# Routing 4,096 tokens to the two experts that they use, beside an attention pass that runs group by group

## The chip, the cores and the metric

One core of a Trainium2 chip. The time is the device time of one execution in microseconds (us), as the median of the runs. The profile is one further execution; its span runs from the first to the last instruction. Engines: PE (TensorE, with PEld for its weight loads), DVE (VectorE), ACT (ScalarE), POOL (GpSimd), SP (SyncE, which issues transfers).

## What is computed

The input x has 8 batches of 512 tokens of 128 numbers, all in float32. Cut to what matters:

```
xn = layernorm(x)
q = rope(xn @ wq);  k = rope((xn @ w_down) @ wk_up);  v = (xn @ w_down) @ wv_up     # 16 heads of 8
scores = q . k / sqrt(8), only keys whose page (32 tokens) is not later than the query's
s = softmax(scores) @ v @ wo
logits = silu(xn @ rw1 + rb1) @ rw2 + rb2          # 8 experts
w = softmax over the two largest logits, 0 elsewhere
y = xn + sum over experts e of w[e] * (silu(xn @ ew1[e] + eb1[e]) @ ew2[e] + eb2[e])   # hidden width 256
out = x + s * silu(y)
```

So only two of the eight experts have a weight that is not zero for a token.

## The kernel before

A token tile is 128 tokens, a batch has TT = 4 of them. The 16 heads form NG = 4 groups of GH = 4 heads. Every engine walks the same list of named steps in one order, and semaphores join them. The list is made of an opening, then for each of the 8 batches a stage B (`stage_b`) and a stage C (`stage_c`); steps in `AHEAD` are done for the next batch, those in `FINAL` for the one before.

Stage B is the expert half. For each of the 8 experts and both halves of the hidden width, `layer1` forms a 128x512 product as three FP32R terms (high x high, low x high, high x low, in `split_product`), ACT applies Silu into `eh`, and `layer2` multiplies each of the 4 token tiles by the second weights; DVE adds it to `acc` with the token's weight `gate_w`. All experts run on all tokens. Between them TensorE forms row scores for the softmax's maxima of groups 1 to 3 (`max_scores`), each of which DVE reduces, and turns the maxima (`neg_max_t`) so that a transfer can put them into rows of `q_stack`, where they are subtracted inside the score product. The choice of the two experts (`top_two`, `weights`) runs once per batch on DVE.

Stage C is the attention half: 12 steps of `scores` (key-major products into a ring of 4 PSUM banks), exp on ACT into `probs`, and `pv`. Around them stand the projections of the next batch (`proj`, three terms each), rope (DVE multiplies, `split` into high and low), the transfers that stack q and k (`stack` on SP), the head copies (`heads` on DVE for groups 0 and 1, `act_head` on ACT for the others) and the maxima of group 0 for the next batch (`max0`). A ring `ring` of 4 banks, two banks `wide` and two banks `misc` hold all products. POOL only forms 1/sqrt(var) and the last addition.

Of the kernel before, what the change touches and what calls it, by code (L numbers as in the profile page):

```python
# [7 lines left out]
F32R = mybir.dt.float32r  # L27
ALU = mybir.AluOpType
# [3 lines left out]
P = 128  # L32
# [10 lines left out]
NPAIR = TT * (GH // 2)  # L43
NMAX = (NG - 1) * NPAIR
NMAX0 = TT * GH
NSTEP = NG * 3
NEXP = GH // 2
# [4 lines left out]
DVE_GROUPS = 2  # L52
NACT = (NG - DVE_GROUPS) * GH
NTOP = 11
MAX_SLOT = 8
EH_RING = 6


def stage_b():

    maxima, top = iter(range(NMAX)), iter(range(NTOP))
    max_steps = (1, 1, 2, 2, 2, 2, 2, 2, 2, 2, 1, 2, 1, 1, 1, 0)
    layer2_at = {4: 0, 6: 1, 7: 2, 9: 3, 11: 4, 13: 5, 15: 6}
    extra = {0: [("logits", 0)], 1: [("gate", 0)], 2: [("out_rows", 0)], 3: [("tanh", 0), ("out_rows", 1)],
             4: [("weights", 0), ("neg_max", 0)], 5: [("out_rows", 2), ("negate", 1)],
             6: [("weights_t", 0)], 7: [("out_rows", 3)], 8: [("neg_max", 1), ("stats", 0)], 9: [("out_cols", 0)],
             10: [("negate", 2)], 11: [("project", 0)], 12: [("neg_max", 2), ("norm", 0)],
             15: [("negate", 3)]}
    seq = [("router", 0)]
    for s in range(NL1):  # L70
        seq.append(("layer1", s))
        if s == NL1 - 1:
            seq += [("x_cols", 0), ("exp_table", 0)]
        for _ in range(max_steps[s]):
            seq.append(("max", next(maxima)))
            if s >= 1:
                seq += [("top", n) for _, n in zip(range(3), top)]
        seq += extra.get(s, [])
        if s < NACT:
            seq.append(("act_head", s))  # L80
        if s in layer2_at:
            seq.append(("layer2", layer2_at[s]))
    assert not list(maxima) and not list(top)
    return seq + [("layer2", NE - 1), ("neg_max", 3), ("proj", 0), ("expert_bias", 0), ("proj", 1)]


def stage_c():

    before_pv = {5: [("heads", 0)], 8: [("heads", 1)]}
    after_pv = {0: [("proj", 2), ("split", 0), ("proj", 3)], 1: [("split", 1), ("stack", 0)], 4: [("stack", 1)],  # L90
                7: [("stack", 2)], 10: [("stack", 3)], NSTEP: [("values", 0), ("negate", 0)]}
    for n in range(NMAX0):
        at = 6 + n * 6 // NMAX0
        (after_pv if n * 6 % NMAX0 >= 12 or at == 8 else before_pv).setdefault(at, []).append(("max0", n))
    seq = []
    for n in range(NSTEP + 1):
        if n < NSTEP:
            seq.append(("scores", n))
        seq += before_pv.get(n, [])
        if n >= 1:  # L100
            seq.append(("pv", n - 1))
        seq += after_pv.get(n, [])
    return seq


STAGE_B, STAGE_C = stage_b(), stage_c()
FINAL = ("gate", "out_rows", "out_cols", "project")
AHEAD = [s for s in STAGE_B if s[0] in ("stats", "norm", "x_cols", "proj")] + [
    s for s in STAGE_C if s[0] in ("proj", "split", "stack", "values", "heads", "max0", "negate")]
MISC = ("router", "logits", "layer2", "out_rows", "out_cols", "project", "weights_t", "neg_max",  # L110
        "expert_bias", "x_cols", "proj", "values", "max0")


def opening():

    seq = [s for s in AHEAD if s[0] in ("stats", "norm", "x_cols", "proj", "values")]
    seq += [("split", 0), ("split", 1), ("stack", 0), ("stack", 1), ("stack", 2), ("stack", 3), ("router", 0),
            ("layer1", 0), ("layer1", 1), ("logits", 0)]
    top = iter(range(NTOP))
    seq += [("top", n) for _, n in zip(range(5), top)] + [("heads", 0)]  # L120
    for n in range(NMAX0):
        seq.append(("max0", n))
        if n in (3, 7):
            seq.append(("layer1", 2 + n // 4))
        if n == 7:
            seq.append(("heads", 1))
        if n >= 8:
            seq += [("top", n) for _, n in zip(range(1), top)]
    return seq + [("negate", 0)]


OPENING = opening()


def steps_of(first=False, last=False):
    return [s for s in STAGE_B + STAGE_C
            if not (first and (s[0] in FINAL or s in OPENING and s not in AHEAD)) and not (last and s in AHEAD)]


def misc_jobs(steps):  # L140

    jobs = [s for s in steps if s[0] in MISC]
    assert len(jobs) % 2 == 0
    return jobs


JOBS = {name: misc_jobs(steps) for name, steps in (
    ("prologue", OPENING), ("first", steps_of(first=True)), ("middle", steps_of()),
    ("last", steps_of(last=True)), ("epilogue", [s for s in STAGE_B if s[0] in FINAL]))}
PER_BATCH = len(JOBS["middle"])  # L150
# [4 lines left out]
def build(nc, x, wq, w_down, wk_up, wv_up, wo, rw1, rb1, rw2, rb2, ew1, eb1, ew2, eb2,  # L155
          cos_t, sin_t, ident_c, key_rows, query_rows, head_mask, rank_c, out):
    ctx = ExitStack()
    with ctx:
# [118 lines left out]
        def batch_of(step, b):  # L277

            return b - 1 if step[0] in FINAL else b + 1 if step in AHEAD else b

# [739 lines left out]
```

## Time and profile before

| | us |
|---|---|
| median of 3 runs | 667.03 (665.81 to 667.17) |
| span of the profiled execution | 663.7 |
| PE busy | 607.3 |
| DVE busy | 467.0 |
| ACT busy | 354.4 |
| POOL busy | 18.6 |

The median of the runs is 3.3 us above the profiled span, which is the part of an execution outside the first and the last instruction. Busy PE time counts pipelined products with their whole duration, so two consecutive starts say more of a product's price than its duration does. Names in the rows are cut: digits at the end of a name are left out, so `ew_sb` is `ew2_sb`.

### The profile page before, as it was taken

The page shows a single profiled execution, that of the slowest core. Times are in us where ns is not written, and L with a number is a line of the kernel's source. Part 1 is how long each engine was busy: PE and PEld are TensorE (multiplying, and loading weights), DVE is VectorE, ACT ScalarE, POOL GpSimd, SP SyncE. Part 2 cuts the span into 40 slices and gives each one's busy share as a digit, 9 for nine tenths or more (in the row PEclk, how much of TensorE's full clock was granted, in tenths as well). Part 3 has the DMA queues.
Part 4 walks back from the last instruction along what each step waited for, and adds up shares of the span by engine and source line. Part 5 has one row for each costly group of instructions (what it writes and reads, how often), then busy time and mean ns, then how long its engine had stood idle before and what let it go on. Part 6 is the DMA issues. An engine that isn't in the chain of part 4 may idle for free.

```text
span 663.7 us, 12438 instructions
## 1 busy us (share of the span) xinstructions
PE 607.3 (92%) x4116; PEld 448.6 (68%) x4116; DVE 467.0 (70%) x1199; ACT 354.4 (53%) x507; POOL 18.6 (3%) x20
## 2 busy tenths in 40 slices
PE   2569999999999999999999999999999999999895
PEld 1448855787567865678557875788656885578643
DVE  6677866787568866798667865698757875687502
ACT  2123456643766347754576438653576445763573
POOL 0000000000000100001000000001000000000000
PEclk9758999999999989999999999999999998999999
DMA  5810002100120002200021001200021001200000
GB/s 170 210 43 2 3 13 61 27 1 19 38 60 1 18 1 49 46 1 18 21 51 25 1 18 45 50 1 18 1 67 28 2 17 25 51 22 2 19 1 16
DMA packets 21798, 20.93 MB, mean 32 GB/s; under 512 B 4545, under 2 KB 14450, under 8 KB 21778
## 3 DMA queue, kind: packets, MB, share of 16 engines
q1 hardware_dynamic: 21778, 20.67, 12.9%
q8 instruction: 12, 0.20, 0.1%
q14 instruction: 8, 0.07, 0.0%
HBM read 5.45 MB, written 2.10 MB: 11 GB/s over the span
## 4 chain that ended last, share of the span: by engine, by line
PE 70%; DVE 13%; issue 12%; ACT 2%; SPq 1%; DMA 1%; DVEq 0%; POOLq 0%; POOL 0%; ACTq 0%
PE bank L500 15%; PE bank L580 10%; PE ring L517 7%; PE ring L562 7%; PE bank L446 5%; PE bank L447 5%; PE bank L448 5%; PE bank L517 5%; DVE row_max L861 5%; PE ring L565 2%; DVE acc L908 2%; PE ring L566 2%; PE bank L462 1%; ACT probs L683 1%; PE bank L478 1%
## 5 line engine op out<-in xcount | busy, mean ns | idle before, releaser
L683 ACT ACTIVATE probs<-ring 128x768 f32<-128x768 f32 (+1 forms) x192 | 158.9, 880 | 79.7 <-PE ring L562 48.8
L861 DVE TENSOR_REDUCE row_max<-ring 128x2 f32<-128x256 f32 (+1 forms) x192 | 152.3, 819 | 13.1 <-PE ring L517 13.0
L643 ACT ACTIVATE eh<-bank,bias_cols 128x512 f32<-128x512 f32 x128 | 87.8, 686 | 136.9 <-PE bank L448 134.9
L500 PE MATMUL bank<-ew_sb,eh 128*128 128x128 f32 x1024 | 125.8, 276 | 2.4 <-DVE x_lo L786 2.4
L500 PEld LDWEIGHTS bank<-ew_sb,eh 128*128 128x128 f32 x1024 | 120.1, 192 | 5.6 <-issue 3.8
L517 PE MATMUL ring<-k_head,q_stack 108*128 108x256 f32 (+2 forms) x384 | 93.4, 344 | 12.3 <-DVE row_max L861 11.2
L517 PEld LDWEIGHTS ring<-k_head,q_stack 108*128 108x128 f32 x384 | 66.7, 194 | 37.0 <-DVE row_max L861 24.8
L580 PE MATMUL bank<-probs,v_cols 128*32 128x512 f32 (+3 forms) x1024 | 88.0, 442 | 0.4 <-ACT probs L683 0.4
L908 DVE SCALAR_TENSOR_TENSOR acc<-bank,gate_w,acc 128x128 f32<-128x128 f32 x224 | 63.1, 345 | 32.3 <-PE bank L500 32.1
L856 DVE TENSOR_REDUCE row_max<-bank 128x1 f32<-128x128 f32 (+3 forms) x128 | 58.9, 487 | 32.6 <-PE bank L517 31.7
L562 PE MATMUL ring<-q_stack,k_head 128*128 128x512 f32 (+1 forms) x256 | 71.8, 395 | 3.5 <-ACT probs L683 3.5
L562 PEld LDWEIGHTS ring<-q_stack,k_head 128*128 128x128 f32 x256 | 43.1, 193 | 28.5 <-ACT probs L683 19.3
L446 PE MATMUL bank<-x_hi,ew_hi 128*128 128x512 f32 x128 | 59.4, 464 | 2.1 <-DVE bias_cols L749 2.1
L447 PE MATMUL bank<-x_hi,ew_lo 128*128 128x512 f32 x128 | 51.7, 404 | 0.0
L448 PE MATMUL bank<-x_lo,ew_hi 128*128 128x512 f32 x128 | 51.7, 404 | 0.0
L891 DVE COPY o_cols<-bank 128x512 f32<-128x512 f32 x32 | 22.1, 692 | 39.5 <-PE bank L580 39.5
L517 PE MATMUL bank<-k_head,q_stack 108*128 108x256 f32 (+2 forms) x128 | 43.1, 392 | 4.6 <-DVE k_head L884 3.0
L668 ACT ACTIVATE k_head<-k_stack,hmask 128x512 fp32r<-128x512 f32 x64 | 45.4, 712 | 0.0
L517 PEld LDWEIGHTS bank<-k_head,q_stack 108*128 108x128 f32 x128 | 24.6, 202 | 30.4 <-DVE row_max L856 18.5
L580 PEld LDWEIGHTS bank<-probs,v_cols 128*32 128x32 f32 x1024 | 23.4, 108 | 30.0 <-issue 10.5
L884 DVE TENSOR_SCALAR k_head<-k_stack,hmask 128x512 fp32r<-128x512 f32 x64 | 26.7, 482 | 13.5 <-DMA k_stack<-roped_lo 13.5
L565 PEld LDWEIGHTS ring<-q_stack,k_head 128*128 128x128 f32 x128 | 24.1, 188 | 15.1 <-ACT probs L683 15.1
(115 smaller groups left out, 659.4 us busy)
## 6 DMA issues: line engine op xcount, KB each, us to landing
k_stack<-roped_hi SPq DMA_DIRECT2D x64, 64.0 KB, 2.0
q_stack<-roped_hi SPq DMA_DIRECT2D x64, 64.0 KB, 2.0
k_stack<-roped_lo SPq DMA_DIRECT2D x32, 64.0 KB, 2.0
q_stack<-roped_lo SPq DMA_DIRECT2D x32, 64.0 KB, 2.0
out<-out_sb SPq DMA_DIRECT2D x8, 256.0 KB, 2.3
x_all<-in_L_attn_x SPq DMA_DIRECT2D x4, 448.0 KB, 6.9
probs<-in_L_ffn_ew SPq DMA_DIRECT2D x1, 1024.0 KB, 5.8
q_stack<-neg_rows SPq DMA_DIRECT2D x32, 16.0 KB
```

Of the source, the lines that this page charges most:

```text
L446: mm(ps, w_hi, x_hi[:], start=True, stop=False)
L447: mm(ps, w_lo, x_hi[:], start=False, stop=False)
L448: return mm(ps, w_hi, x_lo[:], start=False, stop=True)
L500: last = mm(ps[:, t * E:(t + 1) * E], eh[:, s % EH_RING, t * P:(t + 1) * P], ew2_sb[:, e, f, :], start=(f == 0), stop=(f == HALVES - 1))
L517: return mm(ps[:, 0:width], q_stack[0:MAX0, g, i * P:(i + 1) * P], k_head[0:MAX0, GH * g + r, 0:width], start=True, stop=True)
L562: mm(ring[:, r, j * P:T], k_head[:, h, j * P:(j + 1) * P], q_stack[:, g, j * P:T], start=True, stop=True).then_inc(st_full, 1)
L580: last = mm(wide[g % 2][32 * r:32 * r + 32, dst:T], v_cols[:, tile, GH * g + r, :], probs[:, n % 2, r, src:src + T - dst], start=(tile == ...
L643: nc.scalar.activation(eh[:, s % EH_RING, :], wide[s % 2][:], ACT.Silu, bias=bias_cols[:, s:s + 1]).then_inc(hidden_done, 1)
L683: nc.scalar.activation(probs[:, n % 2, r:r + 2, lo:T], ring[:, r:r + 2, lo:T], ACT.Exp, scale=SCALE).then_inc(exp_done, 1)
L856: V.tensor_reduce(row_max[:, 0, i, r:r + 1], ps[:, 0:(i + 1) * P], AX, ALU.max).then_inc(max0_done, 1)
L861: V.tensor_reduce(row_max[:, g, i, 2 * pair:2 * pair + 2], ring[:, 2 * (m % 2):2 * (m % 2) + 2, 0:(i + 1) * P], AX, ALU.max).then_inc(max_ ...
L908: ins = stt(out=acc[:, t, :], in0=ps[:, t * E:(t + 1) * E], scalar=gate_w[:, t, e:e + 1], in1=(xn if e == 0 else acc)[:, t, :], op0=ALU.mu ...
```

## The change

The whole order is laid out anew, with no loops in the program.

1. Attention: after an opening, 32 windows, one for each group of each batch. In a window there are three score steps; between the two halves of each stand two of the next windows' maxima (a list `MAXIMA` gives six per group, each two banks wide). The head copies, negated maxima, projections, rope and output work fill fixed places (`fills`). Six PSUM banks form one ring for nearly all products; a product waits for whoever read its banks last.
2. Projections and router are single float32 products in place of three FP32R terms.
3. All tokens are normalised, and the router runs for all 8 batches, in the opening. The choice of experts runs once for all 32 token tiles. DVE counts and TensorE sums ranks, which give each token two slots in a list of 39 tiles of 256 slots, in which a tile belongs to one expert. POOL scatters the normalised rows into it in DRAM (64 indirect transfers).
4. ACT issues transfers that pack each expert's weights and biases in DRAM and that fill the slot list with zeros first.
5. In each of the windows 9 to 18 a burst of 4 tiles runs: SP loads each tile's expert (its number read from `tile_e`) and its slots, TensorE turns them and runs both layers in float32, SP stores the results to DRAM.
6. From window 20 on POOL gathers two rows per token (64 indirect transfers), and from window 23 DVE adds them to xn with the two weights.
7. s is stored to DRAM for each batch and fetched at the end with x; silu, the product and the addition run for all batches at the end.

The diff, cut to its core:

```diff
-NPAIR = TT * (GH // 2)
-NMAX = (NG - 1) * NPAIR
-NMAX0 = TT * GH
+MAXIMA = ((0, (0, 1, 2, 3)), (1, (0, 1, 2, 3)), (2, (0, 1)), (2, (2, 3)), (3, (0, 1)), (3, (2, 3)))
+NBANK = 6
+BT = B * TT
+ROWS = 256
+NTILE = (2 * B * T + NE * (ROWS - 1)) // ROWS
+BURST = 4
+W_RING = 2 * BURST
+NBURST = -(-NTILE // BURST)
...
+def opening():
+
+    seq = [("prep", 0, 0), ("stats", 0, 0), ("norm", 0, 0), ("x_cols", 0, 0), ("proj", 0, 0), ("proj", 0, 1),
+           ("split", 0, 0), ("split", 0, 1)]
+    seq += [("stack", 0, g) for g in range(NG)]
+    seq += [("consts", 0, 0), ("router", 0, 0), ("stats", 1, 0)] + [("norm", b, 0) for b in range(1, B)]
+    seq += [("x_cols", 1, 0), ("values", 0, 0), ("logits", 0, 0), ("heads", 0, 0)]
+    for b in range(1, B):
+        seq += ([("x_cols", b + 1, 0)] if b + 1 < B else []) + [("router", b, 0)] + maximum(0, b - 1)[:b <= NM]
+        seq += [("logits", b, 0)]
...
+def window(b, g, route):
...
+    ahead = [maximum(w + 1, 4) + maximum(w + 1, 5), maximum(w + 2, 0) + maximum(w + 2, 1),
+             maximum(w + 2, 2) + maximum(w + 2, 3)]
...
+    if burst == -1:
+        seq += [("load", i, k) for i in (0, 1) for k in tiles_of(i)]
+    if GATHER_FROM <= w < GATHER_FROM + B:
+        seq.append(("gather", w - GATHER_FROM, 0))
+    for k, fill in enumerate(fills(b, g)):
...
+        seq += [("scores", b, 2 * n)] + ahead[k][0:1] + [("scores", b, 2 * n + 1)] + ahead[k][1:2]
...
+    if run:
+        seq += [("silu_table", burst, 0), ("layer1", burst, 0), ("layer1", burst, 1), ("layer2", burst, 0),
+                ("layer2", burst, 1), ("exp_table", burst + 1, 0), ("store_rows", burst, 0)]
+        if burst + 2 < NBURST:
+            seq += [("load", burst + 2, k) for k in tiles_of(burst + 2)]
...
+            def load(burst, k):
+
+                if k == 0:
+                    sp.wait_ge(s_pack, 16 * 6)
+                    sp.wait_ge(tiles_ready, 1)
+                    sp.wait_ge(scattered, 16 * 2 * BT)
...
+                expert = sp.value_load(tile_e[0:1, k:k + 1], min_val=0, max_val=NE - 1)
+                sp.dma_start(w_ring[:, k % W_RING, :],
+                             w_pack[bass.ds(expert, 1)].rearrange("o p w -> (o p) w")).then_inc(w_in_ring[k % W_RING], 16)
...
+            def proj(b, which):
...
+                for term in range(2):
+                    last = mm(ps[:, term, :], w_att[:, 2 * which + term, :], x_col[:, b % 2, :], start=True, stop=True)
...
+            def layer1(burst, q):
...
+                for c in halves_of(burst, q):
+                    for f in range(HALVES):
+                        last = mm(ps[:, c % 2, f * ROWS:(f + 1) * ROWS], w_ring[:, BURST * (burst % 2) + c, f * P:(f + 1) * P],
+                                  slots_t[:, c * ROWS:(c + 1) * ROWS], start=True, stop=True)
...
+            def consts(b, n):
+
+                act.dma_start(w_pack[:, :, 0:HID], ew1).then_inc(s_pack, 16)
...
+                act.wait_ge(prep_pool, 2)
...
+                for a in range(0, per, ZERO):
+                    n = min(ZERO, per - a)
+                    act.dma_start(flat[:, a:a + n], blank[:, 0:n]).then_inc(zeroed, 16)
...
+            def norm(b, n):
...
+                for t in range(TT * b, TT * b + TT):
+                    last = activation(xn[:, t, :], x_all[:, t, :], ACT.Identity, scale=rstd[:, t:t + 1],
+                                      bias=shift[:, t:t + 1])
...
+            G.memset(v_cols[:], 0.0).then_inc(prep_pool, 1)
+            G.memset(probs[:], 0.0).then_inc(prep_pool, 1)
...
+            def scatter(b, n):
+
+                pool.wait_ge(place_ready, 1)
+                pool.wait_ge(zeroed, 16 * -(-(NTILE * ROWS // P * E) // ZERO))
+                pool.wait_ge(xn_ready, B)
+                for t in range(BT):
+                    for which in range(2):
+                        G.indirect_dma_start(slot_rows, bass.IndirectOffsetOnAxis(ap=place[:, which, t:t + 1], axis=0),
+                                             xn[:, t, :], None).then_inc(scattered, 16)
```

## Rows read from the trace of the kernel before

**Rows 1.** The page: busy us and share of each engine; tenths in 40 slices.

```profile
PE 607.3 (92%) x4116; PEld 448.6 (68%) x4116; DVE 467.0 (70%) x1199; ACT 354.4 (53%) x507; POOL 18.6 (3%) x20
...
PE   2569999999999999999999999999999999999895
...
PEclk9758999999999989999999999999999998999999
```

**Rows 2.** The page's chain that ended last, shares by engine.

```profile
PE 70%; DVE 13%; issue 12%; ACT 2%; SPq 1%; DMA 1%; DVEq 0%; POOLq 0%; POOL 0%; ACTq 0%
```

**Rows 3.** Windows: length, busy of PE, PEld, DVE, ACT, POOL, clock, DMA, GB/s.

```profile
10.00:20.00 10.00, 5.58 (x20) 4.21 (x20) 6.75 (x19) 1.16 (x1) 0.00 (x0) 1.00 0.86 245
...
203.00:237.40 34.40, 32.84 (x226) 28.49 (x224) 29.73 (x82) 15.65 (x26) 2.30 (x2) 1.00 0.04 9
244.00:273.00 29.00, 28.74 (x217) 16.93 (x216) 18.16 (x37) 20.98 (x25) 0.00 (x0) 0.95 0.18 41
629.30:648.10 18.80, 17.97 (x145) 8.78 (x144) 2.08 (x3) 14.83 (x19) 0.00 (x0) 1.00 0.00 1
```

**Rows 4.** Timeline of TensorE in one expert half: start, us, what.

```profile
206.57 1.95 PE L500 MATMUL bank<-ew_sb,eh 128*128 128x128 f32 x16
208.28 0.48 PE L446 MATMUL bank<-x_hi,ew_hi 128*128 128x512 f32 x1
...
209.07 0.64 PE L517 MATMUL ring<-k_head,q_stack 108*128 108x256 f32 x4
209.55 0.60 PE L590 MATMUL bank<-ident,o_cols 128*128 128x128 f32 x4
209.91 0.48 PE L446 MATMUL bank<-x_hi,ew_hi 128*128 128x512 f32 x1
```

**Rows 5.** Timeline of TensorE at the bias product and what follows it.

```profile
241.78 1.12 PE L513 MATMUL bank<-eb_blocks,gate_t 32*128 32x512 f32 x2
242.83 0.51 PE L446 MATMUL bank<-x_hi,w_att_hi 128*128 128x512 f32 x1
```

**Rows 6.** Groups of ScalarE by form: busy us, mean ns, idle before.

```profile
L683 ACT ACTIVATE probs<-ring 128x768 f32<-128x768 f32 x128 | 98.1, 809 | 38.7 <-PE ring L566 30.9 <-PE ring L562 7.7
L643 ACT ACTIVATE eh<-bank,bias_cols 128x512 f32<-128x512 f32 x128 | 87.8, 686 | 136.9 <-PE bank L448 134.9
...
L683 ACT ACTIVATE probs<-ring 128x1024 f32<-128x1024 f32 x64 | 62.1, 1022 | 41.1 <-PE ring L562 41.1
...
L621 ACT ACT_TABLE_LOAD x16 | 20.5, 1283 | 0.3
```

**Rows 7.** Timeline of TensorE in the last batch: the same step of two groups.

```profile
629.27 1.06 PE L580 MATMUL bank<-probs,v_cols 128*32 128x512 f32 x8
...
635.56 1.06 PE L580 MATMUL bank<-probs,v_cols 128*32 128x512 f32 x8
```

**Rows 8.** Groups of VectorE by form.

```profile
L908 DVE SCALAR_TENSOR_TENSOR acc<-bank,gate_w,acc 128x128 f32<-128x128 f32 x224 | 63.1, 345 | 32.3 <-PE bank L500 32.1
...
L861 DVE TENSOR_REDUCE row_max<-ring 128x2 f32<-128x1024 f32 x48 | 57.2, 1220 | 1.7 <-PE ring L517 1.6
...
L884 DVE TENSOR_SCALAR k_head<-k_stack,hmask 128x512 fp32r<-128x512 f32 x64 | 26.7, 482 | 13.5 <-DMA k_stack<-roped_lo 13.5
...
L891 DVE COPY o_cols<-bank 128x512 f32<-128x512 f32 x32 | 22.1, 692 | 39.5 <-PE bank L580 39.5
```

**Rows 9.** Timeline of the opening: POOL's power, SyncE's issue of x.

```profile
5.40 1.02 POOL L962 TENSOR_TENSOR rstd<-var_eps,half_exp 128x4 f32<-128x4 f32 x1 [4.95 <-DVE var_eps L768]
...
12.57 8.94 SPq L380 DMA_DIRECT2D x_all<-in_L_attn_x  x4
```

**Rows 10.** The page's DMA issues: count, KB each, us to landing.

```profile
out<-out_sb SPq DMA_DIRECT2D x8, 256.0 KB, 2.3
```

**Rows 11.** Timeline of the end.

```profile
652.46 0.69 DVE L891 COPY o_cols<-bank 128x512 f32<-128x512 f32 x1 [4.93 <-PE bank L580]
...
660.95 0.38 SPq L412 DMA_DIRECT2D out<-out_sb  x1
```

More of the change, by code:

```diff
@@ L51 @@
 MASK0, MAX0 = 96, 96 + 3 * TT
-DVE_GROUPS = 2
-NACT = (NG - DVE_GROUPS) * GH
+MAX_SLOT = 8
 NTOP = 11
[L55 to L84, printed above, removed]
@@ L106 @@
[L106 to L129, printed above, removed]
@@ L132 @@
[L132 to L149, printed above, removed]
@@ new lines, in build, with take @@
+        done_of = {"x_cols": x_col_ready, "proj": rope_ready, "values": v_ready, "router": r_ready, "logits": logits_read,
+                   "max": max_done, "scores": exp_done, "neg_max": neg_rows_ready, "out_rows": rows_ready,
+                   "out_cols": o_t_ready, "project": s_ready, "ranks": ranks_read, "slots_in": slots_ready,
+                   "layer1": hidden_ready, "layer2": y_ready}
+        def take(pe, step):
+            for prev in FREED[step]:
+                pe.wait_ge(done_of[prev[0]], COUNT[prev])
+            return ring[:, PLACE[step], :]
@@ L350, in build, with wait_full, run, halves_of @@
+        def wait_full(eng, step):
+            eng.wait_ge(slot_full, JOB_AT[step] + 1)
+            return ring[:, PLACE[step], :]
+        def run(do):
+            for kind, b, n in STEPS:
+                if kind in do:
+                    do[kind](b, n)
+        def halves_of(burst, q):
+            return [k % BURST for k in tiles_of(burst) if k % BURST // 2 == q]
         block = ctx.enter_context(nc.Block())
@@ L367, in _ @@
             sp.dma_start(hmask[:], head_mask).then_inc(s_const, 16)
+            for t in range(TT):
+                sp.dma_start(tiles[:, 1:B, t, :], tokens[:, 1:B, t]).then_inc(s_x, 16)
             sp.dma_start(rank[:], rank_c.partition_broadcast(P)).then_inc(s_rw, 16)
@@ new lines, in neg_max_t, with scores @@
+            def neg_max_t(b, g):
+                pe.wait_ge(neg_ready, NG * b + g + 1)
+                ps = take(pe, ("neg_max", b, g))
+                for i in range(TT):
+                    last = turned(ps[0:MAX_SLOT, 0, i * P:(i + 1) * P], neg_max[:, g, i, :], ident[:])
+                last.then_inc(slot_full, 1)
+            def scores(b, e):
+                n, half = divmod(e, 2)
+                g, j = divmod(n, 3)
+                if j == 0 and half == 0:
+                    pe.wait_ge(neg_in[g], 16 * b + 16)
+                ps = take(pe, ("scores", b, e))
+                for r in range(2):
+                    h = GH * g + 2 * half + r
@@ new lines, in layer1, with gate @@
+            def layer1(burst, q):
+                ps = wait_full(act, ("layer1", burst, q))
+                for c in halves_of(burst, q):
+                    for f in range(HALVES):
+                        last = activation(hidden[:, c, f, :], ps[:, c % 2, f * ROWS:(f + 1) * ROWS], ACT.Silu,
+                                          bias=w_ring[:, BURST * (burst % 2) + c, B1 + f:B1 + f + 1])
+                last.then_inc(hidden_ready, 1)
+            def gate(b, n):
+                act.wait_ge(mixed, b + 1)
+                activation(xn[:, TT * b:TT * b + TT, :], xn[:, TT * b:TT * b + TT, :], ACT.Silu).then_inc(gated, 1)
@@ L952, in _ @@
+            run({"prep": prep, "consts": consts, "stats": row_stats, "norm": norm, "proj": proj, "split": split, "heads": heads,
+                 "max": max_scores, "negate": negate, "pv": pv, "values": values, "out_rows": out_rows, "logits": logits,
+                 "top": top_two, "gap": gap, "count": count, "ranks": ranks, "places": places, "weights": weights,
+                 "layer2": layer2, "combine": combine, "result": result})
         @block.gpsimd
```

1133 lines of the change are left out of this document (585 added, 548 removed).

## The prediction

> **What bounds the kernel now.** I read the engine line and the slices of the page first: TensorE is busy 92% of the span, VectorE 70%, and TensorE's granted clock is near its upper level except in the slices from about 33 to 50 us, where it stands at 0.5, that is 1.2 GHz [rows 1]. The chain that ended last is TensorE for 70% [rows 2]. Then the stretches of one batch: in the expert half (34.4 us) TensorE is busy 32.8 us, in the attention half (29 us) 28.7 us, VectorE 29.7 and 18.2 [rows 3]. Busy TensorE time overlaps itself, so I take prices from the starts in the timeline: second-layer products of one expert (16 instructions, 8 float32 products of 128 columns) go from 206.57 to 208.28, 1.71 us, 0.21 each; the three-term first-layer product from 208.28 to 209.07, 0.79; four row-score products of 256 columns 0.48; four transposes 0.36 [rows 4]. A batch so has 16 x 0.79 + 8 x 1.71 = 26.3 us of expert products. TensorE is the bound of both halves.
>
> **The change, part by part.** All counts are from the two sources.
>
> *Experts.* Removed per batch: the 26.3 us above, router 0.8, four logits products (0.86), the weights' transpose and the bias product (1.05, [rows 5]): 29 us, 232 in all. Added: 39 tiles of 256 slots. A tile has 2 transposes (0.18), 2 float32 products of 256 columns (0.21 x 2 each, 0.86) and 4 of 128 columns (0.86): 1.9 us, with some switching 2.1. A burst of four is 8.5 us, 9.75 bursts are 83 us. ScalarE in a burst: one copy of 1,024, eight Silu of 256 (between a third and the whole of 0.69, so 0.43 each) and two table loads (1.28, [rows 6]): 8 us, just inside TensorE's 8.5, if the last exps are done. VectorE's bias additions lie under it.
>
> *Attention.* The last batch runs attention with no maxima ahead: 6.28 us for one group's scores and probs x v [rows 7]. The changed kernel has 32 windows, one group each. To 6.28 come the group's maxima (5,632 columns; at 0.48 for 1,024 it is 2.7 us), the transposes of the maxima 0.36, and a quarter of the batch's values 0.86, transposes 0.36, projections, eight transpose groups of the output (1.44), turning back 0.36 and output product 0.86. The projections change from three FP32R terms (0.79) to one float32 product of 512 columns: four times the 128-column price is 0.86, the bias product's row gives 1.05; I take 0.95, so 3.8 per batch, a loss of 0.6. Sum of the extras 7.7, a quarter 1.9. TensorE needs 6.28 + 2.7 + 0.36 + 1.9 = 11.2 us in a window. VectorE: six reductions (0.69 + 2 x 0.95 + 3 x 1.22 = 6.3; 512 wide is put like the 512-wide copy, 768 midway), a copy 0.69, negations 0.3, a quarter of [rope 2.4, split 3.6, values 0.7, output 1.4, head copies 8 x 0.48] = 3.0: 10.3 us [rows 8]. ScalarE: exps 2 x 1.02 + 4 x 0.81 = 5.3, head copies 8 x 0.69 a batch, copies: 7.5 us [rows 6]. TensorE and VectorE are now nearly equal and meet over three pairs of PSUM banks in one order. VectorE's pieces of 1.2 to 1.9 us (rope, split, heads) stand ahead of reductions that TensorE waits for. Perfect cover would give 11.2; if every such piece were paid, 11.2 + 3.0 = 14.2. Today's halves run at 95% or better of TensorE, with a VectorE that had slack; I take 12.3, 394 us for 32.
>
> *Routing.* Done once, on 128x256 rather than 128x32: about 45 VectorE instructions in windows 0 and 1. By the nearest rows a 128-wide one costs 0.35 and a 512-wide one 0.69 [rows 8], so 0.3 to 0.4: 14 us, of which some 2 are covered. 12 us. *Combining*: eight products of 0.345 per batch, 2.8 us in each of windows 23 to 30 on the nearly full VectorE; half is paid, 12 us.
>
> *Opening.* It now holds normalisation of all 4,096 tokens (28 ScalarE pieces of 128x128, at about 0.345 by VectorE's row, 9.6), eight transposed copies and seven more routers (15 x 0.69, 10.4): 20 us of ScalarE. Ahead of that, in ScalarE's own queue, stand nine DMA issues that write 2.6 MB of packed weights (8 x 128 x 642 x 4 bytes) and 5.1 MB of zeros (39 x 256 x 512 bytes). An issue costs little, but four loads of x issued behind 2 MB held SyncE 8.94 us [rows 9]: an issuer is held while the queues are full. At 245 GB/s [rows 3] 7.7 MB last 32 us. POOL must fill two large tiles before its first power, which came at 5.4 us [rows 9]; that moves everything some 10 us later. From both sides: issues free, 16 (first transposed copy) + 6 (nine issues) + 20 + 6 (exp table, negated maxima and their transfer) = 48 us to the first scores; ScalarE held until all bytes have moved, 16 + 32 + 11 (x and weights, 2.6 MB, ahead in the queues) + 20 + 6 = 85. I take the middle, 68. The SyncE stacks hide beside it.
>
> *Scatter and load.* POOL issues 64 indirect transfers, beginning some 35 us into the windows, and SyncE waits for all of them at window 8 before the first eight loads; behind that wait stand the transfer of the maxima and the copies into the stacks, so a late scatter stops attention. There are some 75 us for it, 1.17 us a transfer. No row shows an indirect transfer. Below: SyncE's direct issue, under 1 us (8.94 / 4 is one that was held). Above: a whole direct transfer to landing, 2.3 [rows 10]. POOL's own smallest instruction takes 1.02 [rows 9]; nearest to that I take 1.2, 77 us, so barely in time. The first eight loads (3.6 MB, 15 us at 245 GB/s) begin only then and TensorE needs half of them at the end of window 9: 10 us for both. The 64 gathers have three windows' lead and 11 windows' time, 2.1 us each, and are hidden. If that cover is gone, VectorE stands at `combine`, with the next reductions queued behind it, and TensorE behind those.
>
> The Trainium skill, "SBUF — State Buffer", section "SBUF: two separate sides", says that descriptors made by GpSimd wait while VectorE copies from SBUF to SBUF in its two-port mode, and gives some 3.1 us for a transfer of 0.62 so overlapped. No row of before bears on it, since no transfer is issued from POOL; by its figure the 64 would be an estimated 198 us.
>
> *End.* Today the last copy of the heads' outputs at 652.46 is followed by the store at 660.95 and the end at 663.7 [rows 11], with one probs x v before: 12 us. The new end adds a store and a reload of s (2.3 each at least), two VectorE passes and gates, less POOL's addition: 18 us.
>
> **Sum.** 68 + 394 + 83 + 12 + 12 + 10 + 18 = 597 us against the span of 663.7. The median of 667.03 lies 3.3 above that span; the same margin gives 600 us, 10% faster. As a check: taking only the 232 us off TensorE and putting 83 + 5 on would give 520, so 80 us of the gain are given back, in the opening, to VectorE and at window 8.
>
> **Rivals.** (A) *It overlaps better*: windows 11.3, opening 50, loads in time: 600 - 32 - 18 - 10 = 540 us. For it: attention halves today lose only 5%. Against: VectorE had 37% slack there. (B) *VectorE and the bank ring set the pace*: windows 13.5 and an opening of 80: 600 + 38 + 12 = 650 us. For it: 10.3 against 11.2 us in one shared order. (C) *The indirect transfers are slow*, the one that ends on the other side: at c us each the scatter is late by 64c - 75 us, and SyncE's wait at window 8 passes that on whole. With c = 2.3, the landing time, it is 72 us late and the gathers 12 more: with the 2 us that 597 already holds, 600 + 70 + 12 = 682 us. It decides from c = 2.2 up. (D) *POOL stands still while VectorE copies between SBUF tiles*: these copies (eight of heads at 0.48 and two casts, put the same, in a batch of 49 us) fill 10% of the time, so 1.2 becomes 1.35 and the scatter 86 us: 610 us. This is the rule of the Trainium skill cited above, at this kernel's own overlap; if POOL were as late as the page's own example, it would be case C.
>
> Chances: forecast 0.50 (its own range 570 to 640), A 0.17, B 0.15, C 0.13, D 0.05. The range that holds all but the outer parts of A and C is 543 to 668. A change of under 0.2% can't be told from none here. Faster 0.85 (all but C, and 0.02 of B for the edge), same 0.02, slower 0.13.
>
> **What would show each step.** In the changed trace: 32 windows of some 12.3 us, 21 where a burst runs; first exps at about 68 us; POOL's scatter instructions' spacing, and whether SyncE's wait on the scatter ends before window 8 would have begun; TensorE's granted clock, which may fall where it waits. It was 1.00 in a stretch of the last batch where TensorE was busy 17.97 of 18.8 us [rows 3], and in the slices of the opening where TensorE had less to do it fell to 0.5 [rows 1]. The prediction is wrong most easily in the opening (bytes through the DMA engines, POOL's fills) and in c.

## The result and the profile after

The changed kernel takes 795.15 us (median of 4 runs, 790.11 to 796.36) against 667.1 (665.81 to 668.49): ratio 1.191 [1.187, 1.196]. It is 19% slower. 600 was forecast, 668 was the upper bound, and of the rivals only the one with slow indirect transfers ended on this side.

The page of the changed kernel, for [rows 1] and [rows 2], and three groups of it (line engine op, tiles | busy us, mean ns | idle before):

```profile
PE 555.1 (70%) x3223; PEld 352.5 (44%) x3223; DVE 389.1 (49%) x696; ACT 335.6 (42%) x500; POOL 135.6 (17%) x141
...
PEclk9658867555599989989999899989588788888987
...
PE 53%; DVE 13%; another core or an unknown queue 12%; ACT 10%; issue 9%; POOL 1%; DMA 1%; DVEq 0%; SPq 0%; ACTq 0%; POOLq 0%
...
L849 DVE TENSOR_REDUCE row_max<-ring 128x4 f32<-128x512 f32 (+2 forms) x192 | 199.2, 1046 | 233.6 <-PE ring L512 152.2
...
L1044 POOL DMA_INDIRECT pair_in<-y_rows,place x64 | 61.5, 961 | 485.3 <-DMA y_rows<-work 347.2
...
L1032 POOL DMA_INDIRECT slot_rows<-xn,place x64 | 62.0, 969 | 102.1 <-DVE place L952 82.9
```

TensorE's busy time did fall, by 52 us, but its share is 70% where it was 92: no engine is the bound over the span. The clock line has a stretch at half level that is not in [rows 1], slices 8 to 11, 140 to 220 us. The chain has a new entry, 12% released by "another core or an unknown queue": on one core this is a wait whose releaser the profile could not name. The timelines write it `<-remote`; below it is called an unnamed wait. The transfers themselves cost 0.96 us each, with 0.30 between them: 1.26, where the forecast had 1.2.

Now the stretch of the scatter, first by stretches of time (columns as in [rows 3]), then the timeline of the changed kernel (start, us, what, in brackets the idle time before it and what ended it):

```profile
122.00:132.00 10.00, 8.19 (x38) 4.64 (x38) 4.82 (x9) 2.20 (x3) 7.61 (x8) 0.66 0.16 48
132.00:142.00 10.00, 2.65 (x21) 1.22 (x20) 2.80 (x4) 2.05 (x2) 7.57 (x9) 0.71 0.17 52
142.00:212.00 70.00, 9.36 (x32) 5.21 (x32) 4.19 (x7) 2.20 (x3) 46.85 (x49) 0.50 0.17 52
```

```profile
135.55 0.86 PE L552 MATMUL wide<-probs,v_cols 128*32 128x256 f32 x16
...
136.34 1.01 PE L532 MATMUL ring<-q_stack,k_head 128*128 128x384 f32 x2
...
161.87 1.15 SPq L389 DMA_DIRECT2D k_stack<-roped_hi  x2
161.87 0.69 DVE L862 COPY o_cols<-wide 128x512 f32<-128x512 f32 x1 [22.22 <-remote]
...
164.25 1.19 PE L512 MATMUL ring<-k_head,q_stack 108*128 108x256 f32 x4 [26.89 <-DVE k_head L843]
...
169.04 0.81 ACT L707 ACTIVATE probs<-ring 128x768 f32<-128x768 f32 x1 [32.06 <-remote]
...
169.91 1.22 PE L512 MATMUL ring<-k_head,q_stack 108*128 108x256 f32 x4 [3.82 <-issue]
...
178.78 0.69 DVE L849 TENSOR_REDUCE row_max<-ring 128x4 f32<-128x512 f32 x1 [14.64 <-remote]
```

From 142 to 212 us every engine but POOL is nearly idle. The products of probs x v at 135.55 should be over by 136.4; VectorE's copy of their result starts at 161.87, and so does SyncE's transfer, 25 us later. The score product of 136.34 reaches ScalarE at 169.04, the maxima product of 164.25 reaches VectorE at 178.78. In the other direction there is no delay: ScalarE's exp ends at 169.85 and TensorE goes on at 169.91. So what TensorE finishes is seen by others 13 to 32 us late, while POOL's transfers run (122.26 to 203.5 us) and for some 9 us after. I call this the hold. It comes back, shorter, at the gathers, as in this row of the changed kernel's timeline:

```profile
563.09 0.81 ACT L707 ACTIVATE probs<-ring 128x768 f32<-128x768 f32 x1 [5.52 <-remote]
```

Whether the products themselves stand still or only their completion is held can't be read here, since their ends are modelled. One thing can: from 147 to 165 us and from 167 to 227 us the trace has no packet of an instruction queue, and VectorE's four long waits end inside these stretches (161.87, 178.78, 195.58 and 212.78 us). So no arrival of late instructions that the trace shows ended them.

### The profile page after: what moved, and what is told of

The parts are those of the page before. It is cut to its first block, busy times and chain, and to the rows that moved or that the text cites. A ratio compares the mean times of both kernels' runs of the same rounds, so it can differ in the third digit from the quotient of the medians.

```text
span 792.2 us, 9060 instructions
## 1 busy us (share of the span) xinstructions
PE 555.1 (70%) x3223; PEld 352.5 (44%) x3223; DVE 389.1 (49%) x696; ACT 335.6 (42%) x500; POOL 135.6 (17%) x141
## 4 chain that ended last, share of the span: by engine, by line
PE 53%; DVE 13%; another core or an unknown queue 12%; ACT 10%; issue 9%; POOL 1%; DMA 1%; DVEq 0%; SPq 0%; ACTq 0%; POOLq 0%
PE ring L512 10%; PE wide L552 10%; PE ring L532 5%; PE ring L607 5%; PE ring L472 4%; ACT probs L707 4%; DVE row_max L849 3%; PE ring L597 3%; PE ring L520 3%; PE ring L535 2%; PE ring L536 1%; ACT xn L662 1%; PE ring L588 1%; ACT slots_t L723 1%
## 5 line engine op out<-in xcount | busy, mean ns | idle before, releaser
L849 DVE TENSOR_REDUCE row_max<-ring 128x4 f32<-128x512 f32 (+2 forms) x192 | 199.2, 1046 | 233.6 <-PE ring L512 152.2
L512 PE MATMUL ring<-k_head,q_stack 108*128 108x256 f32 (+2 forms) x512 | 143.9, 391 | 115.8 <-issue 50.1
L1044 POOL DMA_INDIRECT pair_in<-y_rows,place x64 | 61.5, 961 | 485.3 <-DMA y_rows<-work 347.2
L552 PE MATMUL wide<-probs,v_cols 128*32 128x512 f32 (+3 forms) x1024 | 108.8, 524 | 0.4 <-ACT probs L707 0.4
L1032 POOL DMA_INDIRECT slot_rows<-xn,place x64 | 62.0, 969 | 102.1 <-DVE place L952 82.9
L535 PE MATMUL ring<-q_stack,k_head 128*128 128x256 f32 x128 | 41.8, 346 | 17.6 <-ACT rows L686 9.6
L607 PE MATMUL ring<-area,work 128*128 128x128 f32 x312 | 37.5, 278 | 1.4 <-ACT work L729 1.4
L607 PEld LDWEIGHTS ring<-area,work 128*128 128x128 f32 x312 | 35.6, 192 | 5.0 <-ACT work L729 5.0
L472 PE MATMUL ring<-x_col,w_att 128*128 128x512 f32 x64 | 35.7, 689 | 1.6 <-DVE row_max L849 0.9
L597 PE MATMUL ring<-slots_t,area 128*128 128x256 f32 x156 | 35.8, 382 | 0.0
```

The lines of the kernel that those rows point to most:

```text
L472: last = mm(ps[:, term, :], w_att[:, 2 * which + term, :], x_col[:, b % 2, :], start=True, stop=True)
L512: last = mm(ps[:, at // T, at % T:at % T + width], q_stack[0:MAX0, g, i * P:(i + 1) * P], k_head[0:MAX0, GH * g + r, 0:width], start=True, ...
L535: mm(ps[:, r, 0:2 * P], k_head[:, h, 3 * P:T], q_stack[:, g, 2 * P:T], start=True, stop=True)
L552: last = mm(wide[g % 2][32 * r:32 * r + 32, dst:T], v_cols[:, tile, GH * g + r, :], probs[:, n % 2, r, src:src + T - dst], start=(tile == ...
L597: last = mm(ps[:, c % 2, f * ROWS:(f + 1) * ROWS], w_ring[:, BURST * (burst % 2) + c, f * P:(f + 1) * P], slots_t[:, c * ROWS:(c + 1) * RO ...
L607: last = mm(ps[:, c % 2, a * E:(a + 1) * E], hidden[:, c, f, a * P:(a + 1) * P], w_ring[:, BURST * (burst % 2) + c, HID + f * E:HID + (f + ...
```

## The experiments

Ratios are to the kernel before on the same chip (665.7 to 666.9 us). Six theories follow one another: indirect transfers slow (rival C), a stream of indirect transfers as such, straight code, spread rows, density, and the place of the stream.

**1. Two scatters in place of 64.** The other 62 are left out, so most slots hold zeros, and the loads wait for these two alone.

```diff
-                for t in range(BT):
+                for t in range(1):
                     for which in range(2):
```

> The changed kernel with 2 of its 64 scatter transfers; the other 62 are left out, so most slots keep zeros, while every other instruction stays. Theory S (a stream of indirect transfers from POOL holds back TensorE's completions): the stretch of windows 1 and 2, 85.5 us with the 64 transfers, falls to about 30, the whole to about 720 us. Rival F (the unrolled program's instruction fetch stalls there, whatever POOL does): the stretch stays above 70 us and the whole within 10 us of 795.

680.43 us, ratio 1.022 [1.019, 1.025]: 115 us are the scatter's, more than the 75 that I expected, for the gathers, untouched, hold nothing any more. A kernel that also left out 48 gathers (e2) gave no result, and this one answers what it asked.

**2. All 64, in pairs behind exps.** The complete kernel; eight calls of eight transfers in windows 2 to 9, the bursts two windows later.

```diff
-FIRST_BURST = 9
+FIRST_BURST = 11
...
+    if 2 <= w < 10:
+        seq.append(("scatter", w - 2, 0))
...
-                for t in range(BT):
+                for t in range(TT * b, TT * b + TT):
+                    pool.wait_ge(exp_done, 6 * (b + 2) + (1, 2, 4, 5)[t % TT])
```

> The changed kernel, whole, with its 64 scatters spread over windows 2 to 9, two at a time, each pair behind an exp of its window, the bursts two windows later (11 instead of 9), gathers two later, combination one window earlier behind them. Theory S in the form that a queue must build up (12 transfers went by before TensorE lagged): the hold almost vanishes, 720 to 735 us. S in the form that each transfer costs TensorE its share: the same some 60 us are spread out, 780 us or more.

685.71 us, ratio 1.030 [1.027, 1.033], below both expectations: 109 us come back with all 64 transfers in place. No wait of over 1 us for an unnamed releaser is left, although the first 16 gathers still run back to back from 517 to 537 us.

**3. The same stream in the kernel before, at first put badly.** 16, then 48 indirect transfers to rows that follow each other in a spare tensor, in each of 7 rounds, behind POOL's 1/sqrt(var); the 48 also with the middle rounds written out straight.

```diff
+                if later(b, 1):
+                    for k in range(48):
+                        G.indirect_dma_start(spare, bass.IndirectOffsetOnAxis(ap=row_no[:, k:k + 1], axis=0),
+                                             x_all[:, 0, k % TT, :], None).then_inc(spare_done, 16)
+                    pool.wait_ge(spare_done, 768 * b)
```

> The kernel before, whole, with 16 indirect scatters of 128 rows from a constant tile to a spare DRAM tensor, issued back to back by POOL in each of 7 rounds (20 us of each 76 us). It has loops, and nothing reads what they write. Theory S: TensorE is held for the last part of each stream, 5 to 12 us a round, 35 to 85 us in all. Rival F: no more than 10 us.

> The kernel before, whole and with its loops, with 48 indirect scatters to a spare tensor back to back in each of 7 rounds (61 us of each 76). Theory S (a long stream of indirect transfers alone holds TensorE's completions): each round is held 30 us or more after the first dozen, over 850 us. Rival F (what is held is the fetching of instructions that are not yet on the core, so a kernel whose program is a loop hardly feels it): under 700 us, with more in the first and last rounds, which are straight code, than in the loop.

> As the loop with 48 scatters a round, but with the six middle rounds written out as straight code; same work, same order. Theory S: the same time as the looped one within 3%. Rival F: clearly slower than the looped one, by 30 us or more in each of the six middle rounds, 850 us or more.

673.99 us (1.012 [1.009, 1.015]) with 16, inside the 10 us of the rival; 923.05 (1.386 [1.381, 1.391]) and 916.5 (1.376 [1.370, 1.382]) with 48. The last two look like proof that a stream is enough. They are not. Two views of the kernel with 48 and loops, POOL's timeline and the waits of one round:

```profile
208.46 0.95 POOL L968 DMA_INDIRECT spare<-x_all,row_no  x1 [0.30 <-issue]
210.97 1.25 POOL L976 TENSOR_TENSOR out_sb<-gated,x_all 128x512 f32<-128x512 f32 x1 [1.55 <-DMA spare<-x_all,row_no]
```

```profile
DVE k_head L887 <- DMA k_stack<-roped_lo: 41.4, 1, 41.4
...
PE ring L565 <- DMA q_stack<-neg_rows: 33.8, 1, 33.8
```

The final addition of a round stood behind my stream in POOL's queue; SyncE waited for it with the store, and behind the store stood the stacks and the maxima. All these waits have a named releaser, a DMA: an ordinary queue, of my making, and no hold. The two kernels say only that loops and straight code do the same here, within 1%.

**4. The stream put where nothing stands behind it.** The same 48, behind that addition; rows 48 apart, rows in order, then rows 48 apart and 64 apart in straight code.

```diff
                 G.tensor_tensor(out_sb[:], gated[:], x_all[:, b, :, :], ALU.add).then_inc(out_ready, 1)
+                if not (isinstance(b, int) and b == B - 1):
+                    for k in range(48):
+                        G.indirect_dma_start(spare, bass.IndirectOffsetOnAxis(ap=row_no[:, k:k + 1], axis=0),
+                                             x_all[:, 0, k % TT, :], None).then_inc(spare_done, 16)
+                    pool.wait_ge(spare_done, 768 * (b + 1))
...
+            G.iota(row_no[:], pattern=[[1, 48]], base=0, channel_multiplier=48,
```

> The kernel before with 48 indirect scatters to a spare tensor in each of 7 rounds, each to 128 rows that lie 48 rows apart, issued right behind GpSimd's addition of the projection (at 152 us of the second round), so that neither that addition nor a store stands behind them: GpSimd is free again (some 61 us later) before the next round needs it. If scattered rows hold TensorE: waits of 5 to 30 us of VectorE and ScalarE for finished matmuls in each round, and 750 us or more. If only a stream in the changed kernel holds it: within 2% of 666 us.

> The same with rows that follow each other. If the pattern of the rows matters this one stays within 2% of 666 us while the strided one is slow; if a stream of indirect transfers back to back holds TensorE whatever the rows, both are slow; if neither, both are near 670 us (16 a round cost 1.2%, so 48 may cost 2 to 4%).

> The kernel before with its middle rounds written out, and 48 scatters to rows 48 apart behind the projection's addition in 7 rounds. With loops this took 688 us with no hold. The changed kernel differs from it in that its engines run straight code. If straight code together with rows that lie apart makes the hold: above 750 us with waits for matmuls of 5 us and more. If not: 680 to 695 us.

> The kernel before, written out straight, with 48 scatters a round to the same row numbers as the strided one of the changed kernel that was held (64 rows apart) in a spare tensor of the same size. With 48 rows apart it took 690 us and was not held. If the distance of the rows decides, above 750 us; if something else of the changed kernel does, 685 to 695 us.

688.31, 688.12, 690.43 and 691.44 us. In none is there an unnamed wait of over 1 us. With rows in order POOL's seventh addition comes at 612.83 us, as before the change at 612.78, and VectorE's last product at 658.97 for 658.89. The span grows by 22.8 us only behind that: 16.3 are the last addition, which stands behind the seventh stream (675.93 for 659.66), and 6.5 lie behind the last store's issue and weren't traced. The stretch of the stream in the kernel with rows 64 apart:

```profile
150.00:215.00 65.00, 62.38 (x436) 44.43 (x435) 47.13 (x119) 39.65 (x57) 46.96 (x48) 1.00 0.26 77
```

TensorE is busy 96% beside 48 transfers at the same pace. The expectations of 750 us and more, by rows, by straight code or by their distance, all failed. A dense stream of indirect scatters, to rows apart, beside busy engines, in straight code, holds nothing by itself.

**5. Plain transfers, rows in order, rows apart, another tensor, in the changed kernel.** In all four the experts work on other rows than the routed ones (zeros in the last); the amount of work is the same. Plain transfers of 64 KB; indirect ones to rows in order; to rows 64 apart; the routed rows of a spare tensor.

```diff
-G.indirect_dma_start(slot_rows, bass.IndirectOffsetOnAxis(ap=place[:, which, t:t + 1], axis=0),
+G.dma_start(slot_rows[P * (2 * t + which):P * (2 * t + which) + P, :],
...
```

```diff
-G.indirect_dma_start(slot_rows, bass.IndirectOffsetOnAxis(ap=place[:, which, t:t + 1], axis=0),
+G.indirect_dma_start(slot_rows, bass.IndirectOffsetOnAxis(ap=row_no[:, 2 * t + which:2 * t + which + 1], axis=0),
...
+            G.iota(row_no[:], pattern=[[P, 2 * BT]], base=0, channel_multiplier=1,
```

(64 apart: `pattern=[[1, 2 * BT]]`, `channel_multiplier=2 * BT`.)

```diff
-G.indirect_dma_start(slot_rows, bass.IndirectOffsetOnAxis(ap=place[:, which, t:t + 1], axis=0),
+G.indirect_dma_start(spare_rows, bass.IndirectOffsetOnAxis(ap=place[:, which, t:t + 1], axis=0),
```

> The changed kernel with its 64 indirect scatters replaced by 64 plain transfers of the same 64 KB from POOL to fixed rows, back to back; the slots then hold other tokens than they should, and all else is the same. If it is the transfers made by POOL in general: still about 790 us. If it is the indirect form with its 128 scattered rows: about 690 us.

> The changed kernel, where each of the 64 indirect scatters goes to 128 rows that follow each other (its own block of slot_rows) in place of the routed places. The experts then work on the wrong tokens; the times of all other steps are unaffected. If the hold of TensorE comes from rows that lie scattered in DRAM, it goes and the time is about 690 us (as with the paced scatter, 686). If the indirect form itself, back to back in this kernel, makes the hold, it stays at 785 to 800 us.

> The changed kernel with its 64 scatters back to back, each to 128 rows that lie 64 rows (32 KB) apart, in place of the routed places (the experts then work on the wrong tokens). With rows that follow each other this kernel took 682.7 us and TensorE was not held. If rows that lie apart hold it, 780 us or more, with waits of 14 to 32 us of VectorE and ScalarE for matmuls between 122 and 207 us. If it needs just the routed places, 680 to 690 us.

> The changed kernel with its scatters to the routed places, but into a spare tensor of the same size (the experts read zeros). If the hold comes from the routed row numbers, 785 to 800 us. If it comes from where slot_rows lies in DRAM or from its having been zeroed just before, 680 to 690 us.

Plain 679.68 (1.021 [1.016, 1.026]), in order 682.7 (1.025 [1.022, 1.029]), 64 apart 793.8 (1.184 [1.176, 1.191]), the spare tensor 786.1 (776.67 and 795.52, two runs). The plain ones came denser still, 64 in 35.1 us; they went to rows in order, so a plain transfer to spread rows stands untested. Among the indirect ones the pace is the same and only the row numbers decide. Where they are spread, VectorE's waits for the maxima product and the next are nearly those of the changed kernel (14.64 and 16.11 us): 14.64 and 16.11 with rows 64 apart, 14.51 and 16.11 into the spare tensor. The stretches of the kernel with rows in order, against those shown above, and its later ones:

```profile
122.00:132.00 10.00, 8.46 (x39) 4.74 (x40) 5.24 (x9) 3.50 (x5) 7.68 (x8) 0.67 0.16 48
132.00:142.00 10.00, 7.37 (x43) 4.02 (x43) 6.00 (x11) 2.85 (x4) 7.75 (x8) 0.67 0.35 94
142.00:204.00 62.00, 51.73 (x324) 30.77 (x324) 40.63 (x58) 30.07 (x40) 46.70 (x49) 0.92 0.28 79
...
155.07:215.49 60.42, 50.32 (x324) 29.57 (x320) 39.67 (x57) 29.47 (x39) 36.71 (x38) 0.92 0.27 75
248.40:485.10 236.70, 211.85 (x1325) 147.81 (x1327) 112.00 (x179) 140.99 (x222) 5.35 (x6) 0.92 0.38 105
485.10:624.46 139.36, 114.95 (x724) 69.15 (x716) 96.84 (x164) 67.41 (x89) 45.61 (x48) 0.91 0.21 53
```

The first 10 us are nearly the same in both, the stream included; from 142 us on TensorE has 51.73 us of work in 62 here and 9.36 in 70 there.

**6. The routed rows at half the pace.** The complete kernel, with a power of 128x4 on POOL after each transfer.

```diff
                                              xn[:, t, :], None).then_inc(scattered, 16)
+                        G.tensor_tensor(pause[:, 2 * t + which, :], var_eps[:, 0:TT], half_exp[:, 0:TT], ALU.pow)
```

> The changed kernel, complete, where GpSimd does a power of 128 x 4 into a spare tile (about 1.0 us) after each of its 64 scatters, so that they come one each 2.3 to 2.6 us and not each 1.26. If the hold needs the dense stream, it goes and the time is 685 to 700 us; if each transfer holds TensorE for a time of its own, the hold is the same in sum, spread over 160 us, and the time stays at 780 or more.

727.35 us, ratio 1.092 [1.084, 1.099]: neither of the two expectations, but between them. No unnamed wait is left, with a transfer each 2.31 us, so the hold is gone. The scatter now ends at 269 us, and SyncE stands in front of the first loads with the maxima behind it. This is rival C's mechanism, alone:

```profile
228.00:270.00 42.00, 9.06 (x52) 4.90 (x44) 6.89 (x10) 1.94 (x3) 37.84 (x37) 0.66 0.10 30
```

**7. The dense stream, later.** The complete kernel, 64 transfers back to back, begun behind a chosen exp (the 31st, 9th and 13th; the step stands in window 5, 1 and 2), bursts from window 12, each combining one window after its gather. All three differ only in the start.

```diff
+                pool.wait_ge(exp_done, 6 * 5 + 1)
                 for t in range(BT):
```

> The changed kernel, complete, with its 64 scatters as dense as in it (one each 1.26 us) but begun only behind the first exponential of window 5 (about 155 us, where the TensorE clock is mostly at its upper level), the bursts from window 12 and the combining one window after its gather. If a dense stream to the routed rows holds TensorE wherever it stands: waits of 14 to 30 us from 155 us on and 760 us or more. If the hold hangs on the place (windows 1 to 3, half clock), none, and 690 to 705 us.

> The late dense scatter (685.5 us, no hold, first transfer at 179 us) with its start moved ahead to behind the ninth exponential (about 133 us, 10 us later than in the changed kernel). If the hold hangs on the place of the stream in the first windows: waits of 10 us and more and 760 us or more, as in the changed kernel. If it needed just what stands at 122 to 131 us: none, and 685 us.

> The same with the start behind the thirteenth exponential (about 145 us). If each place before window 4 or 5 is bad: a hold, 740 us or more. If only the first microseconds of the stream in the changed kernel's place are: none, 685 us.

Behind the 31st exp it began at 178.94 us: 685.46 us (1.029 [1.022, 1.035]), no hold. Behind the 9th it could begin as soon as the places were ready, at 119.3 us: 790.48 (1.186 [1.174, 1.198]), so this one doesn't test a later start. Behind the 13th it began at 133.6: 796.41 (1.195 [1.186, 1.203]). I had reckoned with 155, 133 and 145. Two stretches of the late one and then three of the one begun at 133.6, whose last transfer ends at 214.6:

```profile
179.00:189.00 10.00, 6.58 (x43) 3.33 (x44) 7.33 (x11) 5.15 (x8) 7.87 (x8) 0.72 0.32 82
...
199.00:260.00 61.00, 50.21 (x329) 30.25 (x329) 40.49 (x58) 30.07 (x40) 46.67 (x48) 0.96 0.31 86
```

```profile
133.00:143.00 10.00, 7.22 (x49) 4.23 (x49) 6.13 (x11) 2.83 (x4) 7.26 (x8) 0.83 0.31 82
...
153.00:225.00 72.00, 6.12 (x24) 2.60 (x24) 4.29 (x6) 3.29 (x4) 46.91 (x49) 0.50 0.15 46
...
214.70:224.40 9.70, 0.00 (x0) 0.00 (x0) 0.00 (x0) 0.00 (x0) 0.00 (x0) 0.50 0.02 7
```

In all three that are held the stream runs some 8 us beside a busy TensorE first, and then the hold stays, past the end of the stream. The last row shows it: no transfer is issued any more, the DMA engines are busy 2%, and TensorE, VectorE, ScalarE and POOL stand still for 9.7 us. In the five held kernels the last unnamed wait of the scatter ends 9.3 to 9.9 us after its last transfer. So neither a full DMA engine nor a busy POOL is needed at that moment; the hold looks like a backlog that is still being worked off, which no run here shows directly. The clock at the start doesn't sort them: 0.66 and 0.83 in those that were held, 0.67 in the one with rows in order, 0.72 in the late one. That a dense stream holds wherever it stands was wrong, and that only what stands at 122 to 131 us in the changed kernel makes the hold was wrong too.

**8. A version from what the runs showed.** Complete: scatters behind single exps in windows 2 to 8 with bursts from window 10, gathers paced like them, loads four at a time and behind the maxima's transfer, projections one window earlier, and the second 1/sqrt(var) ahead of the first split.

```diff
-                for t in range(BT):
+                for k, t in enumerate(range(BT * b // 7, BT * (b + 1) // 7)):
+                    pool.wait_ge(exp_done, 6 * (b + 2) + k + 1)
...
+                    if b < B - 1:
+                        pool.wait_ge(exp_done, min(NEXP * B, 6 * (GATHER_FROM + b) + (1, 2, 4, 5)[t]))
...
-        if burst + 2 < NBURST:
-            seq += [("load", burst + 2, k) for k in tiles_of(burst + 2)]
+        if k == 1 and -1 <= burst < NBURST - 1:
+            seq += [("load", burst + 1, t) for t in tiles_of(burst + 1)]
```

> The changed kernel, whole, with five edits: scatters in pairs behind exps in windows 2 to 8, bursts from window 10; gathers in pairs likewise; a burst's loads issued after the maxima's transfer of the window before, four at a time; the projections of a batch one window earlier (so that they don't share a window with the output work and the split); the statistics of batches 1 to 7 ahead of the first split. From the 685.7 us with paced scatters: 8 for the opening, 5 to 10 for SyncE's queue, 0 to 15 for the even windows; 655 to 672 us. If windows are long by the order inside a step and not by their load, the last term is nothing: 668 to 675.

660.65 us (656.11 to 664.73), ratio 0.990 [0.985, 0.994]. It beats both kernels, the one before by 1%. What each of the edits beyond the pacing gave of the 25 us from 685.71 was not separated.

## Why the prediction was wrong

The step that failed most is "Scatter and load": it priced POOL's time and what SyncE waits for, and put nothing, without a reason, for what 64 transfers do to an engine that doesn't wait for them. That is 113 us of the 195. The other 82 are sizes, most of them of the window, and they alone would have made the prediction wrong: with rows in order and no hold the kernel takes 682.7 us, slower than before and above the 668 of the range. So the second step that failed is the 12.3 us of a window, which measured 15.1. Ends of stretches are the starts of the maxima's transfers; "no hold" is the kernel with rows in order, in which all of this work is done.

| stretch | forecast | no hold | changed |
|---|---|---|---|
| opening, to the first scores | 68 | 83 | 83.5 |
| windows 0 and 1 with routing | 36.6 | 41.9 | 42.0 |
| windows 2 to 9, first loads | 108.4 | 123.5 | 195.3 |
| windows 10 to 19, bursts | 206 | 236.7 | 236.8 |
| windows 20 to 28, combining | 119.7 | 139.4 | 175.8 |
| the rest | 57.9 | 54.2 | 58.8 |
| span | 597 | 678.7 | 792.2 |

*Scatter* (c = 1.2, in time at window 8): the size was right, 1.26 us, done at 203.5 us, before window 8. The effect was another. The hold costs 72 us in windows 2 to 9 and 41 from the gathers on, where it is seen only in kernels that had it in the scatter. Not all of the 41 are waits: in windows 20 to 28 TensorE's own busy time is 130.8 us for 115.0, at a granted clock of 0.81 for 0.91.

*Rival C* ended on the right side for the wrong reason; its price per transfer was not there, and its mechanism shows only in run 6, where I made it. *Rival D*: VectorE's head copies do lengthen a transfer. In the kernel with rows in order those beside the head copies (134.7 to 136.4, 149.9 to 151.5 and 196.4 to 198.2 us) take 1.05 to 1.22 us in place of 0.96, four of 64 and under 1 us together; the casts, which rival D counted too, lengthen none. The Trainium skill, "SBUF — State Buffer", section "SBUF: two separate sides", has transfers from GpSimd wait for such copies; the direction agrees, but rival D's 9 us were ten times too much.

*Windows* (12.3 us): 15.1 without experts. The row from 155.07 holds four windows: TensorE 12.6 us in each (11.2 forecast), VectorE 9.9 (10.3), ScalarE 7.4 (7.5). Of TensorE's 1.4 above the forecast 1.0 is the clock, 0.92 there where the prices came from rows at 1.00 [rows 3, 4]: 11.2 / 0.92 = 12.2. The other 0.4 wasn't traced. The rest of the window, 2.5 us, is idle. In the timeline of the same kernel:

```profile
195.06 1.15 SPq L390 DMA_DIRECT2D k_stack<-roped_hi  x2
...
196.41 1.76 DVE L844 TENSOR_SCALAR k_head<-k_stack,hmask 128x512 fp32r<-128x512 f32 x4
...
198.27 0.71 PE L513 MATMUL ring<-k_head,q_stack 108*128 108x256 f32 x4 [2.73 <-issue]
...
199.43 0.81 ACT L708 ACTIVATE probs<-ring 128x768 f32<-128x768 f32 x1 [2.98 <-PE ring L533]
```

Four head copies of VectorE stand ahead of the maxima, TensorE waits 2.7 us for them, and ScalarE 3.0 behind TensorE. The forecast named this ("pieces stand ahead of reductions that TensorE waits for"), with 14.2 us if every such piece were paid, and took a third of the 3.0 between. Over the four windows TensorE is idle for 10.1 us where such pieces were priced at 12: 5.4 in two stops like this one (the other is 2.63 us at 212.30), 2.6 in two behind the maxima. So most of it was paid, and at a lower clock. Rival B (13.5 and 80: 650) was nearest to this part.

*Bursts*: 23.7 - 15.1 = 8.6 us a burst, 8.5 forecast. Right, and TensorE is busy 90% of that stretch. Two slips changed nothing: ScalarE's parts of a burst add up to 7.0 us, not 8, and the middle of the opening's bounds is 66.5, not 68.

*Opening* (68): 83, near the upper bound of 85, but not for its reason. ScalarE's timeline in the changed kernel:

```profile
13.72 0.59 ACT L668 COPY x_col<-ring 128x512 f32<-128x512 f32 x1 [5.97 <-PE ring L463]
13.72 0.69 ACTq L642 DMA_DIRECT2D w_pack<-in_L_ffn_ew  x1
...
15.73 5.72 ACTq L646 DMA_DIRECT2D w_pack<-in_L_ffn_eb  x1
...
32.62 4.89 ACTq L654 DMA_DIRECT2D slot_rows<-probs  x3
37.61 0.69 ACT L674 ACTIVATE slots_t<-ring,rb_col 128x512 f32<-128x512 f32 x1 [23.31 <-issue]
39.42 10.88 ACT L662 ACTIVATE xn<-area,shift,rstd 128x128 f32<-128x128 f32 x28 [1.12 <-POOL shift L1023]
...
56.54 0.59 ACT L668 COPY x_col<-ring 128x512 f32<-128x512 f32 x1 [2.91 <-PE ring L463]
58.25 0.69 ACT L674 ACTIVATE slots_t<-ring,rb_col 128x512 f32<-128x512 f32 x1 [1.12 <-PE ring L486]
```

And two stretches of the same kernel, the first of one batch, the second of two:

```profile
56.54:61.84 5.30, 5.30 (x19) 4.05 (x19) 1.42 (x2) 1.27 (x2) 0.00 (x0) 0.50 0.00 0
...
66.00:72.38 6.38, 5.64 (x33) 3.93 (x32) 2.57 (x4) 2.55 (x4) 0.00 (x0) 1.00 0.01 3
```

The issues hold it 23 us (6 in the one bound, 43 in the other; that full queues are the reason, as the prediction has it, no row shows), the normalisation takes 10.9 (9.6), and then the routers run at TensorE's pace, with its transposes, router products and first maxima: 5.3 us a batch at a granted clock of 0.50, where it is busy without a gap, and 3.2 at 1.00. I had added up only ScalarE's own 1.4. From 50.2 to 76.7 us they take 26.5 where 10.4 stood; these 16 us are the term that was missing.

## What to carry to other kernels

Price a background stream twice: its own engine's time, and a test of it beside the busiest engine, at its real place and density. Here pacing 64 indirect transfers behind single exps gave back 109 us of 115 without any transfer fewer. Then check the forecast without the surprise: here 82 us were still missing. When a suspect is planted in another kernel, look first at what stands behind it in its queue; a named releaser in the waits told a queue from a hold here.

## What the runs showed of the hardware

An indirect transfer of 128 rows of 512 bytes occupies POOL for 0.96 us and comes each 1.26 us, the same for scatter and gather and for any rows; 64 plain transfers of 64 KB were all issued in 35.1 us. A dense stream of scatters can make TensorE's completions 13 to 32 us late (41 in the kernel begun at 119.3 us, where ScalarE goes on at 175.38 with a product of 133.59), until 9 to 10 us after the stream. In the changed kernel it was seen only with all three of: indirect transfers to spread rows, 1.26 us spacing, and a start between 119 and 134 us; with 2.31 us, rows in order, plain transfers (to rows in order) or a start at 179 us there was none. What joins the three is open. Straight code, the target tensor and the clock at the start are ruled out as the cause by themselves; a start between 134 and 179 us, and the held kernel's later gathers without its scatter's hold, were not separated further.
